# Where the column maxima of an attention kernel stand in its product steps: none in the score banks while there are four or fewer

## The reference

```python
# layer 0
xn  = layer_norm(x)
q, k, v = xn @ q_w + q_b, xn @ k_w + k_b, (xn @ v_w + v_b) * mask     # 16 heads of 16
att = softmax(q k^T + mask term, over the 1024 keys)
y   = att v
scale, shift = split(silu(cond) @ emb_w + emb_b)
x   = x + silu(layer_norm(y) * (1 + scale) + shift) @ out_w + out_b
# layer 1: q = softmax over the 32 channels of a head, k = softmax over the tokens
att = k^T v per head;  y = q att;  the same modulation, silu and output product
```

## Time and profile before

| | us |
|---|---|
| median of 3 runs | 594.04 |
| lowest, highest | 592.26, 595.14 |
| the profiled execution's own time | 595.13 |
| its span | 593.3 |

### The profile page before, as it was taken

How to read it: one execution, slowest core, us unless ns; L and a number is a source line. 1 busy time by engine, 2 the same in 40 slices (tenths; PEclk the granted TensorE clock), 3 DMA queues, 4 the chain that set the end, 5 groups by cost and what they waited for, 6 DMA issues and landing times. The chain is left out here.

```text
span 593.3 us, 8459 instructions
## 1 busy us (share of the span) xinstructions
PE 562.8 (95%) x3068; PEld 274.0 (46%) x3068; DVE 447.4 (75%) x873; ACT 337.5 (57%) x410; POOL 127.3 (21%) x219
## 2 busy tenths in 40 slices
PE   8998999999999999999999999999999999979987
PEld 8454453334433343445434434555335443525775
DVE  6588777888888878888898888777888887304643
ACT  2522665555677776644677664665785565680531
POOL 4188100240000826300020320000621020003311
PEclk9999999999999999999999998999999999999999
DMA  4262892667301132230041010010101100000002
GB/s 122 93 144 54 191 272 86 163 151 196 72 28 28 28 58 48 36 72 13 2 83 28 2 29 0 1 29 36 28 23 42 35 3 1 1 1 0 1 1 71
DMA packets 18611, 33.74 MB, mean 57 GB/s; under 512 B 3962, under 2 KB 10482, under 8 KB 17804
## 3 DMA queue, kind: packets, MB, share of 16 engines
q1 hardware_dynamic: 18462, 33.18, 22.8%
q10 hardware_dynamic: 110, 0.03, 0.0%
HBM read 19.29 MB, written 13.52 MB: 55 GB/s over the span
## 5 line engine op out<-in xcount | busy, mean ns | idle before, releaser
L925 ACT ACTIVATE prob<-sT 128x1024 f32<-128x1024 f32 x256 | 247.3, 1022 | 115.8 <-PE sT L1102 115.7
L1289 DVE TENSOR_REDUCE halfmax<-bank 128x1 f32<-128x512 f32 x428 | 271.1, 684 | 48.5 <-PE bank L987 46.8
L987 PE MATMUL bank<-ks,qs 50*128 50x512 f32 x428 | 156.6, 478 | 9.6 <-DVE halfmax L1289 3.7
L1122 PE MATMUL bank<-prob,vp 128*17 128x512 f32 x1024 | 135.5, 601 | 0.7 <-ACT prob L925 0.6
L987 PEld LDWEIGHTS bank<-ks,qs 50*128 50x128 f32 x428 | 62.9, 183 | 128.2 <-DVE halfmax L1289 81.6
L1102 PE MATMUL sT<-qs,ks 52*128 52x512 f32 x512 | 104.6, 422 | 6.2 <-ACT prob L925 4.1
L685 POOL TENSOR_TENSOR rstd<-var,neghalf 128x4 f32<-128x4 f32 x10 | 10.2, 1016 | 290.8 <-DVE var L1213 290.8
L1102 PEld LDWEIGHTS sT<-qs,ks 52*128 52x128 f32 x512 | 52.1, 185 | 25.7 <-ACT prob L925 15.9
L1289 DVE TENSOR_REDUCE halfmax<-sT 128x1 f32<-128x512 f32 x84 | 54.3, 686 | 8.3 <-PE sT L987 7.7
L962 PE MATMUL bank<-w,hT 128*128 128x256 f32 x152 | 39.1, 392 | 0.3 <-ACT hT L847 0.3
L722 POOL TENSOR_TENSOR xs<-xs,bias_rows 128x256 f32<-128x256 f32 x32 | 23.3, 729 | 54.7 <-DMA bias_rows<-in_L_cond_b_out 52.1
(11 more groups left out here) (189 smaller groups left out, 586.6 us busy)
## 6 DMA issues: line engine op xcount, KB each, us to landing
stack_rows<-late SPq DMA_DIRECT2D x12, 512.0 KB, 5.8
qs<-stack_rows SPq DMA_DIRECT2D x30, 192.0 KB, 3.4
ks<-stack_rows SPq DMA_DIRECT2D x14, 384.0 KB
stack_rows<-late SPq DMA_DIRECT2D x17, 256.0 KB, 5.2
xs<-in_x SPq DMA_DIRECT2D x4, 256.0 KB, 3.8
xs<-in_x SPq DMA_DIRECT2D x2, 512.0 KB, 4.1
late<-in_L_cond_emb_w SPq DMA_DIRECT2D x1, 1024.0 KB, 10.8
late<-in_L_cond_W_emb SPq DMA_DIRECT2D x1, 1024.0 KB, 12.7
```

The source lines that it names most:

```text
L925: act.activation(prob[:, c % 2, 2 * u:2 * u + 2, :].rearrange("p j n -> p (j n)"), sT[u][:, :], ACT.Exp).then_inc(exp_done, 1)
L987: last = pe.matmul(o, qs[rows, s % SLOTS, c, t * P:(t + 1) * P], ks[rows, hg, c, half * HALF:(half + 1) * HALF], start=True, stop=True)
L1122: last = pe.matmul(acc[32 * j:32 * j + VW, :], vp[:, b, c, hg * GH + j, :], prob[:, c % 2, 2 * u + two, :], start=(c == 0), stop=(c == NT ...
L1289: dve.tensor_reduce(halfmax[:, s % 2, r, half:half + 1], o, axis=AX.X, op=ALU.max, negate=True).then_inc(u.done, 1)
```

## The change

```diff
         def length(k, count):
-            pe_work = 1.85 + sum(PE_WORK.get(key[0], 1.95) for key in pe_at[k]) + (0.24 if has_product(k) else 0.13) * count
+            pe_work = 1.85 + sum(PE_WORK.get(key[0], 1.95) for key in pe_at[k]) + (0.14 * count + 0.2 * max(0, count - 4) if has_product(k) else 0.13 * count)
...
             if has_product(k):
-                return ([0, 0, 0, 0], [1, 0, 0, 0], [1, 1, 0, 0], [1, 2, 0, 0], [1, 1, 0, 2], [1, 2, 0, 2], [2, 2, 0, 2])[counts[k]]
+                return ([0, 0, 0, 0], [1, 0, 0, 0], [2, 0, 0, 0], [2, 1, 0, 0], [2, 2, 0, 0], [1, 2, 0, 2], [2, 2, 0, 2])[counts[k]]
```

## The result

| | before | after |
|---|---|---|
| median of 4 runs, us | 594.45 | 614.39 |
| lowest, highest | 592.26, 595.14 | 610.01, 618.33 |
| the profiled execution's own time | 595.13 | 610.01 |
| its span, mean clock granted to PE | 593.3, 0.996 | 608.2, 0.994 |

The changed kernel takes 1.0312 times as long, interval 1.0263 to 1.0362: slower, as forecast, but beyond the range, which ended at 610. The profiled execution is the fastest of the four; it stands 14.9 us above its counterpart, the median 19.9. So there are two amounts to explain: 15 us inside the trace, and 4 to 5 between trace and median. A second set of five runs of the changed kernel, further down, has a median of 610.87.

A forecast was written before the change was run, and what follows sets the result against it. It took leads set by the three-bank ring to bound product steps, and DVE or exponentials and PE plain ones. Product steps +1.9 and plain steps +8.4 gave 605.4 on the profiled 595.13, 604 from the median; range 598 to 609.

The forecast's parts named there:

- The plan: Maxima per step: 24 leave product steps for plain ones, 19 of which go from three to four; no DMA moves.
- The leads behind a product: Product steps: time from PE's first maximum behind a product to its value matmuls, forecast 2.33 in 17, 3.18 in 80.
- The lent pair: Product steps: two maxima in lent score banks cost PE their own 0.43 us and little else; 20 fewer make 8.6.
- Rival A: Faster, 586 us: lent pairs are worth 8.6, leads stay, six-to-five steps give 5.4, new maxima cost 0.25 each; chance 0.18.
- Rival D: Plain steps: the moved maxima fill DVE, 24 x 0.63 = 15.1, and 1.9 from product steps: 611 us; chance 0.07.
- taking 24 maxima out of the product steps gives nothing back: Product steps: the 8.6 us of lent pairs' PE time is eaten by longer leads, +1.9 us in sum.
- 24 x 0.35 = +8.4 us: Plain steps: each of the 24 arriving maxima costs 0.35 us, taken from neighbouring stretches; between 6.0 and 15.1 in all.
- +0.27 each: Steps 55, 79, 91, 95, 103, no large product before: one more ahead, a read wait, a pair less; -0.43 to +0.6.
- the clock was left as before: PE's clock: the sum had no term for further drops, though the profile showed one, in step 83.
- rival C: The forecast's sum plus two or three more drops of PE's clock, some 1.7 us each: 608 us; chance 0.08.

The follow-up runs named there:

- the layout alone: The kernel before with the new product-step layouts for three and four maxima, its old model and counts kept: 598.77 us against 594.81, ratio 1.0065.
- the model alone: The kernel before with the new counts only; four maxima in a product step stay one ahead, one behind, two lent: 591.97 us, ratio 0.9944.
- the last layouts: Five as [1, 1, 1, 2] and six as [1, 1, 2, 2], against the kernel before: with new counts 589.85 us, with old counts 588.10.
- the fourth later: The changed kernel with four maxima as one ahead of the scores, two behind them, one behind the values, nothing lent: 605.46 us, ratio 1.0168.
- the version with five: New-counts kernel with [1, 1, 1, 2] and [1, 1, 2, 2], model charging more only from the sixth maximum: 587.00 us, on another chip 584.77.

## Why the prediction missed

**What held.** The plan, 24 maxima moved. The leads behind a product, to within 0.1 us: 3.20 in step 80 (3.18), 2.30 in 17 (2.33), 1.28 in 104 (1.28), 2.74 in 82 (2.74). Step 81 was 0.3 above (3.49; 3.41 with the layout alone, where no fall stands in it). Where no large product stands ahead, the leads grew more than I had reckoned: from 1.25 to 1.98 in 55 and 79, from 1.33 to 2.49 and 2.96 in 95 and 103. The lent pair is worth its 0.43: steps 52, 53 and 73 gave 0.28, 0.42 and 0.44. Rival A fell with the leads. Rival D named 611, near what was measured, by a price of 0.63 for a moved maximum; the steps show 0.40, so its number is right by luck. The claim that taking 24 maxima out of the product steps gives nothing back *in this layout* held (+2.3 in the trace); the model alone shows that it was the layout, with the old one they give 13.

**The product steps, one by one.** The sum came out near, partly because errors cancelled.

| steps | forecast | measured |
|---|---|---|
| 9; 17 | +1.0 each | +0.50, and 0.47 in step 10 behind it; +0.97 |
| 13, 16, 18 | +0.19 | +0.17, +0.18, +0.15 |
| 56, 82 | +0.30 | +0.30, +0.30 |
| 80; 81 | +1.4; +1.3 | +1.08; +3.16, about 1.5 without the fall |
| 92; 58, 84 | +0.1; -0.1 | +0.07; -0.15, -0.15 |
| 44, 104, 117; 57 | -0.6; -0.7 | -0.59, -0.58, -0.60; -0.73 |
| 55, 79, 91, 95, 103 | +0.27 | -0.33, -0.33, +0.16, -0.07, +0.87 |
| 43, 72, 109, 111, 116 | -0.4 | 0, 0, -0.01, -0.28, +0.14 |
| 107 | +0.6 | -0.15, and 0.87 in step 106 |
| 83; 7 | 0 | -1.59 (the fall gone); -0.36 |

Where a product stands ahead, the forecast is right almost everywhere; where none does, going from six to five gave 0.03 on the mean instead of 0.4.

**First step that failed: "24 x 0.35 = +8.4 us".** The plain steps grew by 12.8. Without the fall in step 77 that is 11.4, 3.0 more than forecast, and it has two parts. The 24 maxima themselves cost 9.5, which is 0.40 each: the 24 steps that took them show it here, the whole plain sum of the model alone shows the same, and the last layouts show 0.41. That makes 1.1 us. The other 1.9 my sum had no term for: the plain step *ahead of* a product step in the new layout pays too. 54, 78, 94 and 102 lost 0.64, 0.64, 0.60 and 0.43, though they hold no more than before (0.4 came back elsewhere). Step 78, PE, the kernel before and then the changed one:

```profile
343.94 0.50 PE L987 MATMUL bank<-ks,qs 50*128 50x512 f32 x1
343.95 0.96 PE L1102 MATMUL sT<-qs,ks 52*128 52x512 f32 x4
```

```profile
353.06 1.13 PE L987 MATMUL bank<-ks,qs 50*128 50x512 f32 x2
353.80 0.87 PE L1102 MATMUL sT<-qs,ks 52*128 52x512 f32 x4
```

Ahead of the scores of step 79 now stand two maxima, in a ring that the transpose of `neg` uses too. The scores start 0.74 us behind the first of them instead of at once, and the exponential that ends step 78 comes 0.64 later. With one maximum ahead (the fourth later) 54, 78 and 94 are back at their lengths of before, so the layout is the cause. I had seen such a wait, but put it into the product steps, as +0.27 each; together with the steps ahead of them 55, 79, 95 and 103 gave +0.31, +0.31, +0.53 and +1.30.

The price of 0.35 came from neighbouring stretches, and one reading was miscounted: steps 32 to 39 hold 26 maxima, not 25, so 1.23/4 = 0.31 for one more, not 0.25. Beyond that a mean over eight steps says little, since the 19 steps that went from three to four differ much: 36, 42, 47, 71, 101 and 108 took the fourth for nothing, 48 and 110 for 0.1 and 0.25, 26, 34, 37, 39 and 45 for 0.4 to 0.6, and 3, 6, 35, 50, 76 and 114 for 0.8 to 1.3. In 35 and 76 the chain of small DVE operations for `neg` stands between the reads; it does too in 27, which took no maximum and lost 0.51. In 50 and 114 there is no such chain, nor in 3 and 6, and for these four I have no cause. Step 35 after:

```profile
197.99 1.29 DVE L1289 TENSOR_REDUCE halfmax<-bank 128x1 f32<-128x512 f32 x2 [0.21 <-PE bank L987]
...
199.31 0.19 DVE L1292 TENSOR_REDUCE negmax<-halfmax 128x16 f32<-128x32 f32 x1
...
199.53 0.22 DVE L1295 CAST cpieces<-negmax 128x16 fp32r<-128x16 f32 x1
...
199.79 0.17 DVE L1297 TENSOR_TENSOR cpieces<-negmax,cpieces 128x16 fp32r<-128x16 f32 x1
199.88 2.48 DVE L1289 TENSOR_REDUCE halfmax<-bank 128x1 f32<-128x512 f32 x4
```

The chain for `neg`, 0.6 us, stands between reads. With four maxima the read that frees PE's bank comes behind it, and the step went from 2.13 to 3.38. In the version with five the chain stands in step 36 instead, and there 36 is the dear one: 3.43 us, and 2.70 in 35.

**Second step that failed: the clock was left as before.** The sum for the trace was 605.4; 610.0 was measured. The plain steps make 3.0 of it, the fall in 77 1.4 and the product steps 0.4 (81's fall and the one gone from 83 about cancel); outside the steps 0.3 came back. The rest of the miss, another 4.4 to 614.4, is between trace and median, and is the clock too. In the four first runs the times are 610.01, 613.67, 615.12 and 618.33 us at mean clocks of 0.994, 0.986, 0.983 and 0.978: 0.5 us for each 0.001, and a straight line within 0.4 us. So of the 10 us between forecast and median the clock makes about 6, more than any other term, and without it the time would have been in the range. My sum had nothing for it. Two or three falls more was rival C, with a chance of 0.08, but I had set it as an alternative to the sum and closed the range at 610, as though it could not come on top of a plain price at its upper half.

The nine runs of the changed kernel have a mean clock of 0.989, against 0.996 of before. Brought to a full clock by lines through the runs of each kernel, before would be at 592.7 and after at 607.1: a loss of 14, and 0.5 to 5.5 from the clock, by which set of runs one takes.

The rule of the Trainium skill (TensorE: Matmul & The Clock Gate, "A second HAM failure mode: psum-queue depth-cycling"), that PE pausing as it cycles through PSUM banks makes the clock fall repeatedly, thus fits better than I gave it credit for: the kernel with the most idle time ahead of ring maxima (18.0) has the lowest mean clock, the three others with the new layout or the fourth behind the values (12.7 to 15.4) have 0.990 to 0.993, and the fall in 81 stands right behind pauses of 1.35 and 1.36. But the order isn't clean: the model alone, at 9.6 us of idle like before, has 0.9965, the old counts in the last layouts, with 3.8, have 0.9948. And shortening exactly those pauses moved the falls without ending them.

The size of the pause doesn't decide either. In the twelve profiled executions the clock falls 17 times within the steps, and at few places: steps 0 to 2 (four executions), 13 (two), 77 (four), 81 or 83 (five), 98 (two). Only two of the 17 have a pause of 1.35 just ahead; with the others the longest pause near is one of 0.3 to 0.8. The smallest stands in the kernel with the fourth maximum later (PE in step 13, and then the stretch of the fall, with the clock in the third column from the end):

```profile
121.83 0.50 PE L987 MATMUL bank<-ks,qs 50*128 50x512 f32 x1 [0.30 <-DVE halfmax L1289]
```

```profile
124.60:128.00 3.40, 3.40 (x6) 1.10 (x5) 2.56 (x9) 0.00 (x0) 3.09 (x5) 0.50 0.93 196
```

In the profile of the layout alone PE pauses for 1.35 in step 81 and the clock stays up; it falls in 83, behind pauses of 0.61 and 0.23.

**What stays open.** What in this kernel makes the clock fall, and why at one of these places in one run and at another in the next. Whether the lent banks or the third maximum's place make the larger part of the product steps' loss. Whether a fourth ring bank would make the two and two layout as good as the lent pair wasn't tried, as no bank is free.

## What to carry to other kernels

Price a change of layout and a change of counts together: alone, the layout cost 4 us and the counts gained 3; together they lost 15 to 20, because the counts put 14 more steps on the layout that is dear. In a small ring of banks look for the first use that needs a bank again ahead of work that could fill the wait, and put that work there: one ahead, one behind, the rest behind the values. Look at the step ahead as well: what stands ahead of the scores is paid there. And when a stretch is moved to where another engine already has work, take its price from steps of the kind it goes to, one by one, not from a mean over eight.

## What the hardware showed that I had not expected

Pauses of PE of 0.3 us were the longest shortly ahead of a fall of its clock, in kernels whose PE is 94 to 95% busy, and a pause of 1.35 us elsewhere passed without one. A fall costs 1.4 us in step 77 and 1.6 in step 83. The falls recur at a handful of steps in kernels with different layouts. The time of one kernel goes with the mean granted clock, 592.1 to 600.1 us over 21 runs of before, at 0.6 us for 0.001 with a scatter of about 1 us. A maximum in a product step costs 0.36 us and in a plain one 0.40, less than DVE's read of 0.68 either way, so both kinds of step still hide a part of it.
